# Linear-attention layers: the two bias matmuls of a key or query fill as a pair of 32-row groups

## The chip, the cores and the metric

The kernel runs on one core of one Trainium2 chip. The metric is the device time in microseconds (us). The engines are PE (TensorE matmul), DVE (VectorE), ACT (ScalarE), POOL (GpSimd) and SP (SyncE, which here only issues transfers). PEld is TensorE's weight load; it runs beside PE.

## The reference

Two transformer layers with adaptive layer norm. The change touches only the attention of the second, eight linear-attention layers on 4096 tokens (16 sequences of 256), 16 heads of 64, model size 128. One layer:

```python
Q  = elu(x @ Wq + bq) + 1                 # [tokens, 1024]
Kf = elu(x @ Wk + bk) + 1
V  = x @ Wv + bv
KV, sumK = sum(Kf * V, axis=1), sum(Kf, axis=1)      # over the tokens of a sequence
att = Q * KV / (Q * sumK + 1e-6)
x = layer_norm(gelu(att @ Wo + bo) + x)
h = gelu(gelu(x @ W1 + b1) @ W2 + b2)
x = layer_norm(h + x)
```

The biases bq and bk are not small (spread 2.0), so they are added in full precision: each is split into three bf16 parts whose sum is the bias.

## The kernel before, in words

`stack_phase` runs the eight layers. Its unit of work is 512 tokens (two sequences); there are 8 units in a layer and 64 in all. Five stages of successive units overlap in one `step`: A (keys, queries and the first half of the sums) of unit t, B (the rest of the sums, and three quarters of the output projection) of unit t-1, C (the last quarter, gelu, layer norm) of t-2, Dn (first feed-forward matmul) of t-3, E (second, layer norm, state written back) of t-4. The order on each engine is written out by hand in its own `step`, and the engines meet at counting semaphores.

For each unit, `keys(t, s, q)` runs four times (q = 0 to 3, each 128 tokens x 1024 features) and `queries(t, s, q)` four times (each 256 features x 512 tokens). Each fills two PSUM banks of 512 columns, `k_ps` or `q_ps`. In a bank three passes with split fp32 operands (hi x hi, hi x lo, lo x hi) are summed, and a fourth matmul adds the bias: the bf16 tile `b3`, 128 rows of which only rows 0 to 2 hold the three parts and the rest hold zeros, against the ones in `ones_b`. So a fill is eight matmuls, of which the fourth and the eighth are the bias. The eighth raises `k_filled` or `q_filled`.

After that ACT takes the exponential of both banks (`exp_keys`, `exp_queries`), and DVE makes the features (`feature_k`; `feature_q` in two instructions) and raises `k_ready` or `q_ready`, for which the next fill of the same banks waits. There is one pair of banks for keys and one for queries.

In a full step PE's order is: keys 0, queries 0, second feed-forward, first feed-forward 0, project 3, first feed-forward 1, sums, first feed-forward 2 and 3, sums, two groups of transposes, **keys 1**, sums, **queries 1**, sums, keys 2, queries 2, transposes, sums, project 0, sums, keys 3, transposes, project 1, queries 3, project 2. `project` q waits for the q-th `attention` of DVE, and that for the reciprocals of ACT (`log_z`, `exp_z`). DVE's order from queries 1 on is: feature_q 1, normalise, sums, attention 0, feature_k 2, sums, attention 1, sums, normalise, feature_q 2, a cast, attention 2, feature_k 3, feature_q 3, attention 3.

At each layer's end (`closing`, seven times in the loop, and once at the start for layer 0) the weights and the bias of the next layer are put in place by `swap`: for keys (k = 0) between feature_k 3 and feature_q 3 of DVE, for queries (k = 1) behind feature_q 3. DVE's part is a copy of three rows x 1024 of `raw_b3` into `b3`, and the subtraction that makes `wqk_lo`. SP loads `raw_qk` and `raw_b3` (from `bias_dram`, [8, 3, 2048]) a layer ahead, three transfers that all count on `raw_qk_in`.

In `causal_attention_phase`, long before the stack, `heads` multiplies with operands of 64 rows: two matmuls, on rows 0 to 63 and on rows 64 to 127, go to two banks one behind the other. The last phase has one matmul on 32 rows (line 2200).

Of the kernel before, what the change touches and what calls it, by code (L numbers as in the profile page):

```python
# [16 lines left out]
BF16 = mybir.dt.bfloat16  # L17
# [6 lines left out]
P = 128  # L24
# [4 lines left out]
CH = HEADS * VAL  # L29
# [11 lines left out]
def start_counters(eng, sems):  # L41

    for s in sems:
        eng.sem_inc(s, 1)
# [1205 lines left out]
def stack_phase(nc, sem, d, g):  # L1250
# [18 lines left out]
    UNIT = 4 * P  # L1269
# [4 lines left out]
    with ExitStack() as ctx:  # L1274
        sb = lambda n, s, t=F32: ctx.enter_context(nc.sbuf_tensor(n, s, t))
# [5 lines left out]
        raw_1 = sb("t_raw_1", [P, FF])  # L1281
        raw_2 = sb("t_raw_2", [P, NF, D])
        raw_ln = sb("t_raw_ln", [P, 2, D])
        raw_b3 = sb("t_raw_b3", [3, 2 * CH], BF16)

        wqk_hi = sb("t_wqk_hi", [P, 2, CH], F32R)
        wqk_lo = sb("t_wqk_lo", [P, 2, CH], F32R)
# [7 lines left out]
        b3 = sb("t_b3", [P, 2 * CH], BF16)  # L1295
        ones_b = sb("t_ones_b", [P, 4 * P], BF16)
# [6 lines left out]
        x_hi = sb("t_x_hi", [P, 2, UNIT], F32R)  # L1303
        x_lo = sb("t_x_lo", [P, 2, UNIT], F32R)
# [23 lines left out]
        k_ps = ps("t_k_ps", [P, CH])  # L1328
        q_ps = ps("t_q_ps", [P, 2 * UNIT])
# [11 lines left out]
        c = {n: sem("t_" + n) for n in names}  # L1341
# [20 lines left out]
        @block.sync  # L1362
        def _(sp):
            start_counters(sp, c.values())
            sp.sem_inc(c["state_t_ready"], PER)
            sp.sem_inc(c["state_ready"], PER)
            sp.dma_start(params[:], d["params"]).then_inc(const_in, 16)
            sp.dma_start(bv_all[:], d["bv"]).then_inc(const_in, 16)
            with sp.Fori(0, LAYERS) as n:

                once, twice, each_chunk = sp.snap(n + 1), sp.snap(2 * n + 1), sp.snap(NC * n + 1)
                sp.wait_ge(c["wqk_ready"], twice)
                sp.sem_inc(free_seen, 1)
                sp.wait_ge(c["b3_ready"], twice)
                sp.sem_inc(free_seen, 1)
                sp.dma_start(raw_qk[:, 0, :], d["wk"][bass.ds(n, 1), :, :].rearrange("a p c -> (a p) c")).then_inc(c["raw_qk_in"], 16)
                sp.dma_start(raw_qk[:, 1, :], d["wq"][bass.ds(n, 1), :, :].rearrange("a p c -> (a p) c")).then_inc(c["raw_qk_in"], 16)
                sp.dma_start(raw_b3[:], g["bias_dram"][bass.ds(n, 1), :, :].rearrange("a p c -> (a p) c")).then_inc(c["raw_qk_in"], 16)
                sp.wait_ge(c["wv_ready"], once)
                sp.sem_inc(free_seen, 1)  # L1380
                sp.wait_ge(c["bv_dot_ready"], each_chunk)
                sp.sem_inc(free_seen, 1)
                sp.dma_start(raw_v[:], d["wv"][bass.ds(n, 1), :, :, :].rearrange("a p k c -> (a p) k c")).then_inc(c["raw_v_in"], 16)
                sp.dma_start(raw_ln[:], d["ln_before"][bass.ds(n, 1), :, :].rearrange("a k c -> (a k) c").partition_broadcast(P)).then_inc(c["raw_v_in"], 16)
                sp.wait_ge(c["wo_ready"], once)
                sp.sem_inc(free_seen, 1)
                sp.dma_start(raw_o[:], d["wo"][bass.ds(n, 1), :, :, :].rearrange("a p k c -> (a p) k c")).then_inc(c["raw_o_in"], 16)
                sp.wait_ge(c["w1_ready"], once)
                sp.sem_inc(free_seen, 1)
                sp.dma_start(raw_1[:], d["w1"][bass.ds(n, 1), :, :].rearrange("a p c -> (a p) c")).then_inc(c["raw_1_in"], 16)  # L1390
                sp.wait_ge(c["w2_ready"], once)
                sp.sem_inc(free_seen, 1)
                sp.dma_start(raw_2[:], d["w2"][bass.ds(n, 1), :, :, :].rearrange("a p k c -> (a p) k c")).then_inc(c["raw_2_in"], 16)

        @block.tensor
        def _(pe):
# [3 lines left out]
            def keys(t, s, q):  # L1400

                pe.wait_ge(c["k_ready"], 4 * t + q + 1)
                for half in range(2):
                    out, cols = k_ps[:, half * 512:(half + 1) * 512], slice(half * 512, (half + 1) * 512)
                    x = slice(q * P, (q + 1) * P)
                    pe.matmul(out, x_hi[:, s, x], wqk_hi[:, 0, cols], start=True, stop=False)  # L1406
                    pe.matmul(out, x_hi[:, s, x], wqk_lo[:, 0, cols], start=False, stop=False)
                    pe.matmul(out, x_lo[:, s, x], wqk_hi[:, 0, cols], start=False, stop=False)
                    last = pe.matmul(out, ones_b[:, 0:P], b3[:, cols], start=False, stop=True)  # L1409
                last.then_inc(c["k_filled"], 1)  # L1410

            def queries(t, s, q):

                pe.wait_ge(c["q_ready"], 4 * t + q + 1)
                for k in range(2):
                    out = q_ps[:, k * UNIT:(k + 1) * UNIT]
                    lo = (2 * q + k) * P
                    pe.matmul(out, wqk_hi[:, 1, lo:lo + P], x_hi[:, s, :], start=True, stop=False)  # L1418
                    pe.matmul(out, wqk_hi[:, 1, lo:lo + P], x_lo[:, s, :], start=False, stop=False)  # L1419
                    pe.matmul(out, wqk_lo[:, 1, lo:lo + P], x_hi[:, s, :], start=False, stop=False)  # L1420
                    last = pe.matmul(out, b3[:, CH + lo:CH + lo + P], ones_b[:], start=False, stop=True)  # L1421
                last.then_inc(c["q_filled"], 1)

            def sums(t, n, k):
# [119 lines left out]
        def _(act):  # L1544
# [13 lines left out]

            def swap(layer, k):

                act.wait_ge(c["raw_qk_in"], 48 * layer + 49)
                act.activation(wqk_hi[:, k, :], raw_qk[:, k, :], ACT.Copy).then_inc(c["wqk_hi_ready"], 1)

            def exp_keys(t, q):
# [94 lines left out]
        def _(dve):  # L1659
# [3 lines left out]
            def swap(layer, k):  # L1663

                cols = slice(k * CH, (k + 1) * CH)
                dve.wait_ge(c["raw_qk_in"], 48 * layer + 49)
                dve.tensor_copy(b3[0:3, cols], raw_b3[:, cols]).then_inc(c["b3_ready"], 1)
                dve.wait_ge(c["wqk_hi_ready"], 2 * layer + k + 2)
                dve.tensor_tensor(wqk_lo[:, k, :], raw_qk[:, k, :], wqk_hi[:, k, :].bitcast(F32), ALU.subtract).then_inc(c["wqk_ready"], 1)

# [574 lines left out]
def program(nc, d, out):  # L2245
    with ExitStack() as ctx:
# [33 lines left out]
        def block1(sem):  # L2280
            with ExitStack() as ctx:
                local = lambda n, s: ctx.enter_context(nc.sbuf_tensor(n, s, F32))
                g["state_t"] = local("state_t", [P, TOKENS // (4 * P), 4 * P])
                g["state"] = local("state", [P, TILES, D + 1])
                stack_entry_phase(nc, sem, d, g)
                stack_phase(nc, sem, d, g)
                stack_exit_phase(nc, sem, d, g)
            top2_phase(nc, sem, d, g)
            store_phase(nc, sem, g, out)
# [50 lines left out]
```

## Time and profile before

| | |
|---|---|
| median of 3 runs | 4040.78 us (4039.62, 4040.78, 4046.01) |
| profiled execution: span from first to last instruction | 4045.9 us; its own time is the 4046.01 of the runs |
| PE / DVE / ACT / POOL busy | 83% / 69% / 56% / 17% |
| stack phase | about 1188 to 3745 us of the span, 64 units |
| a unit in mid-layer | 39.0 us |
| bias matmuls | 1024 (512 for keys, 512 for queries) |

An engine's busy time is the union of its instructions. Matmuls overlap in the records: a 512-column matmul is recorded with 390 to 400 ns, while the next one starts 230 to 240 ns after it. So the cost of a matmul in a stream is the distance from start to start, and not its recorded duration.

### The profile page before, as it was taken

To read this page: it belongs to the slowest core of one execution; us is meant where nothing else is said; L and a number is where in the kernel's file an instruction comes from. 1 tells how busy PE (TensorE), PEld (TensorE's weight loads), DVE (VectorE), ACT (ScalarE), POOL (GpSimd) and SP (SyncE) were. 2 spreads that over 40 slices of the span, in tenths; PEclk is the share of its full clock that TensorE was granted. 3 is DMA by queue.
4 is the path that set the end of the run, shared out by engine and by line. 5 is a ranking of instruction groups with operands and counts; after the bars stand their busy time and mean duration, and the time that the engine had idled before them with its cause. 6 is when DMAs were issued, how large, how long until landed. Compare 5 with 4: busy or idle time off the path is not lost. (4 is left out here: it accounts for less than half of the span.)

```text
span 4045.9 us, 56998 instructions
## 1 busy us (share of the span) xinstructions
PE 3365.3 (83%) x18213; PEld 2365.0 (58%) x18213; DVE 2807.3 (69%) x8434; ACT 2276.1 (56%) x3608; POOL 669.9 (17%) x826
## 2 busy tenths in 40 slices
PE   6998999513339999999999999999999999999664
PEld 5777777413226656666666666565656666666343
DVE  4556555466237787778787778787878777878566
ACT  3444444201127777777676777676767777677420
POOL 0000000104420111112111212111211111211122
PEclk9999999756659999999999999999999999999866
DMA  1000000002310000000000000000000000000000
GB/s 45 0 0 0 0 0 0 14 8 91 41 56 1 1 18 9 4 11 12 7 1 23 7 1 23 7 1 18 9 4 18 9 4 1 1 1 1 6 0 21
DMA packets 31214, 47.81 MB, mean 12 GB/s; under 512 B 3824, under 2 KB 21296, under 8 KB 30960
## 3 DMA queue, kind: packets, MB, share of 16 engines
q1 hardware_dynamic: 25328, 40.52, 3.1%
q0 software_dynamic: 5632, 4.20, 0.8%
q8 instruction: 124, 2.03, 0.2%
q14 instruction: 130, 1.06, 0.1%
HBM read 36.22 MB, written 8.49 MB: 11 GB/s over the span
## 5 line engine op out<-in xcount | busy, mean ns | idle before, releaser
L1432 PEld LDWEIGHTS t_sum_ps<-state,t_feat_k 128*128 128x128 f32 x4096 | 510.2, 192 | 79.2 <-DVE t_kv L1714 54.2
L1443 PE MATMUL t_o_ps<-t_feat_q,t_wo 128*128 128x512 f32 x1024 | 491.7, 603 | 64.0 <-DVE t_feat_q L1702 64.0
L1582 ACT ACTIVATE t_recip<-t_feat_q,t_z_eps,t_sum_k 128x256 f32<-128x256 f32 x1024 | 529.0, 590 | 24.4 <-DVE t_kv_out L1768 14.7
L1432 PE MATMUL t_sum_ps<-state,t_feat_k 128*128 128x129 f32 x4096 | 528.6, 277 | 16.0 <-DVE t_kv L1714 16.0
L1702 DVE SCALAR_TENSOR_TENSOR t_feat_q<-t_feat_q,t_kv_out,t_recip 128x256 f32<-128x256 f32 x1024 | 512.6, 561 | 6.7 <-ACT t_recip L1590 6.7
L1684 DVE SCALAR_TENSOR_TENSOR t_feat_k<-t_exp_k,t_k_ps 128x1024 f32<-128x1024 f32 x256 | 311.1, 1215 | 195.7 <-ACT t_exp_k L1567 195.7
L1567 ACT ACTIVATE t_exp_k<-t_k_ps,t_minus_one 128x1024 f32<-128x1024 f32 x256 | 283.3, 1107 | 274.7 <-PE t_k_ps L1409 274.7
L1572 ACT ACTIVATE t_exp_q<-t_q_ps,t_minus_one 128x1024 f32<-128x1024 f32 x256 | 284.0, 1109 | 186.4 <-PE t_q_ps L1421 186.4
L1418 PE MATMUL t_q_ps<-t_x_hi,t_wqk_hi 128*128 128x512 f32 x512 | 307.2, 600 | 47.6 <-DVE t_feat_q L1690 39.4
L1406 PE MATMUL t_k_ps<-t_wqk_hi,t_x_hi 128*128 128x512 f32 x512 | 289.8, 566 | 42.0 <-POOL t_x_lo L1854 24.0
L1690 DVE SCALAR_TENSOR_TENSOR t_feat_q<-t_exp_q,t_q_ps 128x1024 f32<-128x1024 f32 x256 | 312.6, 1221 | 8.8
L1443 PEld LDWEIGHTS t_o_ps<-t_feat_q,t_wo 128*128 128x128 f32 x1024 | 180.1, 191 | 213.5 <-issue 123.5
L1590 ACT ACTIVATE t_recip<-t_recip 128x1024 f32<-128x1024 f32 x256 | 270.5, 1056 | 6.2
L1714 DVE CUSTOM_DVE_ANT_0 t_junk<-t_sum_ps,t_wv 128x128 f32<-128x128 f32 x1024 | 242.4, 283 | 0.0
L273 ACT ACTIVATE a_probs<-a_pair,a_negmax 128x128 f32<-128x128 f32 x256 | 94.9, 371 | 261.4 <-DVE a_negmax L366 261.4
L1476 PE MATMUL t_m<-t_hid,t_w 128*128 128x512 f32 x512 | 234.8, 602 | 1.9 <-ACT state_t L1649 1.9
L1872 POOL TENSOR_TENSOR t_x_lo<-t_x,t_x_hi 128x512 fp32r<-128x512 f32 x64 | 92.9, 1451 | 799.0 <-DVE t_x_hi L1793 799.0
L1847 POOL TENSOR_TENSOR t_var_eps<-t_moments,t_ln_eps 128x4 f32<-128x4 f32 x128 | 25.7, 201 | 1159.7 <-DVE t_moments L1725 1159.7
L1745 DVE TENSOR_TENSOR t_y<-t_y,t_x 128x512 f32<-128x512 f32 x64 | 44.3, 692 | 242.6 <-ACT t_y L1612 242.6
L1688 DVE TENSOR_SCALAR t_exp_q<-t_exp_q 128x1024 f32<-128x1024 f32 x256 | 181.1, 707 | 39.0 <-ACT t_exp_q L1572 38.7
L1420 PE MATMUL t_q_ps<-t_x_hi,t_wqk_lo 128*128 128x512 f32 x512 | 206.4, 403 | 0.0
L1419 PE MATMUL t_q_ps<-t_x_lo,t_wqk_hi 128*128 128x512 f32 x512 | 205.6, 402 | 0.0
(355 smaller groups left out, 7550.2 us busy)
## 6 DMA issues: line engine op xcount, KB each, us to landing
t_raw_qk<-in_wk SPq DMA_DIRECT2D x8, 512.0 KB
t_raw_qk<-in_wq SPq DMA_DIRECT2D x8, 512.0 KB
t_raw_v<-in_wv SPq DMA_DIRECT2D x8, 512.0 KB, 3.4
t_raw_o<-in_wo SPq DMA_DIRECT2D x8, 512.0 KB, 3.5
t_raw<-in_w SPq DMA_DIRECT2D x16, 256.0 KB, 2.9
x<-in_x SPq DMA_DIRECT2D x4, 512.0 KB, 7.2
tokens_dram<-r_hn SPq DMA_DIRECT2D x8, 256.0 KB, 2.3
e_w_raw<-in_fc_w SPq DMA_DIRECT2D x4, 512.0 KB, 4.2
```

The costliest lines, as they stand in the source:

```text
L1406: pe.matmul(out, x_hi[:, s, x], wqk_hi[:, 0, cols], start=True, stop=False)
L1418: pe.matmul(out, wqk_hi[:, 1, lo:lo + P], x_hi[:, s, :], start=True, stop=False)
L1432: last = pe.matmul(sum_ps[:, at * (D + 1):(at + 1) * (D + 1)], feat_k[:, 2 * n + i, chunk * P:(chunk + 1) * P], rows, start=(i == 0), stop ...
L1443: last = pe.matmul(o_ps[:], wo[:, chunk, :], feat_q[:, s, chunk, :], start=(chunk == 0), stop=(chunk == NC - 1), skip_group_check=True)
L1567: act.activation(exp_k[:], k_ps[:], ACT.Exp, bias=minus_one[:, 0:1]).then_inc(c["k_exp"], 1)
L1572: act.activation(exp_q[:], q_ps[:], ACT.Exp, bias=minus_one[:, 0:1]).then_inc(c["q_exp"], 1)
L1582: last = act.activation(recip[:, q % 2, k * UNIT + n * SEQ:k * UNIT + (n + 1) * SEQ], feat_q[:, s, chunk, cols], ACT.Ln, bias=z_eps[:, 0:1 ...
L1590: act.activation(recip[:, q % 2, :], recip[:, q % 2, :], ACT.Exp, scale=-1.0).then_inc(c["recip_ready"], 1)
L1684: dve.scalar_tensor_tensor(feat_k[:, q, :], exp_k[:], 1.0, k_ps[:], ALU.min, ALU.max).then_inc(c["k_ready"], 1)
L1690: dve.scalar_tensor_tensor(feat_q[:, s, 2 * q:2 * q + 2, :], exp_q[:].rearrange("p (k t) -> p k t", k=2), 1.0, q_ps[:].rearrange("p (k t) ...
L1702: last = dve.scalar_tensor_tensor(a, a, kv_out[:, s, n, chunk:chunk + 1], recip[:, q % 2, k * UNIT + n * SEQ:k * UNIT + (n + 1) * SEQ], AL ...
L1714: last = dve.tensor_tensor_reduce(junk[:, i, :], sum_ps[:, i * (D + 1):i * (D + 1) + D], wv[:, chunk, :], 1.0, 0.0, ALU.mult, ALU.add, kv[ ...
```

## The change

Each fill issues the six fp32 passes of its two banks first and the two bias matmuls behind them. The bias matmul of bank 0 reads rows 0 to 2 of `b3` and `ones_b`, that of bank 1 reads rows 32 to 34: two groups of 32 rows of the array, neither of the full 128. `b3` and `raw_b3` hold the bias twice, at rows 0 and 32, so SP issues one more small transfer in each layer and DVE copies twice in each `swap`.

```diff
-        raw_b3 = sb("t_raw_b3", [3, 2 * CH], BF16)
+        raw_b3 = sb("t_raw_b3", [P, 2 * CH], BF16)
...
-                sp.dma_start(raw_b3[:], g["bias_dram"][bass.ds(n, 1), :, :].rearrange("a p c -> (a p) c")).then_inc(c["raw_qk_in"], 16)
+                for half in range(2):
+                    sp.dma_start(raw_b3[32 * half:32 * half + 3, :], g["bias_dram"][bass.ds(n, 1), :, :].rearrange("a p c -> (a p) c"))\
+                      .then_inc(c["raw_qk_in"], 16)
...  (keys; the three passes of each half only gain skip_group_check=True)
-                    last = pe.matmul(out, ones_b[:, 0:P], b3[:, cols], start=False, stop=True)
+                for half in range(2):
+                    rows = slice(32 * half, 32 * half + 3)
+                    last = pe.matmul(k_ps[:, half * 512:(half + 1) * 512], ones_b[rows, 0:P], b3[rows, half * 512:(half + 1) * 512],
+                                     start=False, stop=True, skip_group_check=True)
...  (queries)
-                    last = pe.matmul(out, b3[:, CH + lo:CH + lo + P], ones_b[:], start=False, stop=True)
+                for k in range(2):
+                    rows, lo = slice(32 * k, 32 * k + 3), CH + (2 * q + k) * P
+                    last = pe.matmul(q_ps[:, k * UNIT:(k + 1) * UNIT], b3[rows, lo:lo + P], ones_b[rows, :],
+                                     start=False, stop=True, skip_group_check=True)
...  (swap of ACT and of DVE)
-                act.wait_ge(c["raw_qk_in"], 48 * layer + 49)
+                act.wait_ge(c["raw_qk_in"], 64 * layer + 65)
...
-                dve.wait_ge(c["raw_qk_in"], 48 * layer + 49)
-                dve.tensor_copy(b3[0:3, cols], raw_b3[:, cols]).then_inc(c["b3_ready"], 1)
+                dve.wait_ge(c["raw_qk_in"], 64 * layer + 65)
+                for half in range(2):
+                    rows = slice(32 * half, 32 * half + 3)
+                    last = dve.tensor_copy(b3[rows, cols], raw_b3[rows, cols])
+                last.then_inc(c["b3_ready"], 1)
```

## Rows read from the trace of the kernel before

**Rows 1.** The page's part 1: busy us (share of the span) and instructions of each engine.

```profile
PE 3365.3 (83%) x18213; PEld 2365.0 (58%) x18213; DVE 2807.3 (69%) x8434; ACT 2276.1 (56%) x3608; POOL 669.9 (17%) x826
```

**Rows 2.** Busy time by stage: PE, PEld, DVE, ACT, POOL; then clock, DMA, GB/s.

```profile
1188.00:3745.00 2557.00, 2406.27 (x11349) 1581.73 (x11350) 2002.68 (x6243) 1826.23 (x2459) 453.95 (x546) 0.99 0.03 8
...
1988.43:2004.28 15.85, 14.80 (x74) 9.56 (x72) 15.78 (x46) 14.22 (x21) 3.35 (x4) 1.00 0.00 0
2009.87:2048.88 39.01, 37.73 (x181) 24.87 (x180) 30.71 (x98) 28.77 (x40) 6.65 (x8) 1.00 0.00 1
```

**Rows 3.** Groups of instructions by line, PE: busy us, mean ns, idle before, releaser.

```profile
L1443 PE MATMUL t_o_ps<-t_feat_q,t_wo 128*128 128x512 f32 x1024 | 491.7, 603 | 64.0 <-DVE t_feat_q L1702 64.0
...
L1421 PE MATMUL t_q_ps<-t_ones_b,t_b 128*128 128x512 bf16 x512 | 203.4, 397 | 0.0
L1409 PE MATMUL t_k_ps<-t_b,t_ones_b 128*128 128x512 bf16 x512 | 202.1, 395 | 0.0
```

**Rows 4.** Timeline of PE, queries 0 of a mid-layer unit: start us, duration us.

```profile
2008.72 0.39 PE L1421 MATMUL t_q_ps<-t_ones_b,t_b 128*128 128x512 bf16 x1
...
2009.65 0.39 PE L1421 MATMUL t_q_ps<-t_ones_b,t_b 128*128 128x512 bf16 x1
```

**Rows 5.** Timeline of PE in the attention phase: 128 rows, 64 rows, 128 rows.

```profile
503.22 0.39 PE L431 MATMUL a_misc<-ident,a_xn 128*128 128x128 f32 x2
503.54 0.49 PE L486 MATMUL a_pair<-a_kv_t,a_q_t 64*128 64x128 f32 x4
503.86 0.60 PE L489 MATMUL a_pair<-a_kv_t,a_q_t 64*128 64x256 f32 x4
504.39 0.40 PE L493 MATMUL a_pair<-mask,ident_b 128*128 128x128 bf16 x4
```

**Rows 6.** Timeline of PEld (weight loads) over the same stretch.

```profile
503.53 0.30 PEld L486 LDWEIGHTS a_pair<-a_kv_t,a_q_t 64*128 64x128 f32 x4 [0.17 <-issue]
...
504.39 0.23 PEld L493 LDWEIGHTS a_pair<-mask,ident_b 128*128 128x128 bf16 x4 [0.33 <-issue]
```

**Rows 7.** Single lines over the whole run: duration ns min/median/max.

```profile
L486 PE MATMUL a_pair<-a_kv_t,a_q_t x512: 272/322/374, 43.0 to 728.9; 64*128 64x128 f32 x171
...
L489 PE MATMUL a_pair<-a_kv_t,a_q_t x512: 376/377/378, 43.3 to 729.2; 64*128 64x256 f32 x171
...
L493 PE MATMUL a_pair<-mask,ident_b x512: 219/219/230, 43.8 to 729.7; 128*128 128x128 bf16 x171
```

**Rows 8.** Timeline of PE, ACT and DVE, mid-layer unit, keys 1 to project 2.

```profile
1982.39 0.48 PE L1406 MATMUL t_k_ps<-t_wqk_hi,t_x_hi 128*128 128x512 f32 x1
...
1987.28 1.11 ACT L1572 ACTIVATE t_exp_q<-t_q_ps,t_minus_one 128x1024 f32<-128x1024 f32 x1 [1.11 <-PE t_q_ps L1421]
...
1988.43 0.69 DVE L1688 TENSOR_SCALAR t_exp_q<-t_exp_q 128x1024 f32<-128x1024 f32 x1 [0.62 <-ACT t_exp_q L1572]
...
2004.34 1.98 PE L1443 MATMUL t_o_ps<-t_feat_q,t_wo 128*128 128x512 f32 x4 [0.94 <-DVE t_feat_q L1702]
```

**Rows 9.** Timeline of DVE and PE at a layer's end (swap).

```profile
2122.31 0.41 DVE L1667 COPY t_b<-t_raw_b 3x1024 bf16<-3x1024 bf16 x1
...
2122.64 1.21 DVE L1669 TENSOR_TENSOR t_wqk_lo<-t_raw_qk,t_wqk_hi 128x1024 fp32r<-128x1024 f32 x1
...
2123.98 0.49 PE L1406 MATMUL t_k_ps<-t_wqk_hi,t_x_hi 128*128 128x512 f32 x1 [0.69 <-DVE t_wqk_lo L1669]
...
2127.22 0.50 PE L1418 MATMUL t_q_ps<-t_x_hi,t_wqk_hi 128*128 128x512 f32 x1 [1.12 <-DVE t_wqk_lo L1669]
```

**Rows 10.** The same view of SP, start of the stack phase.

```profile
1171.51 0.27 SPq L1378 DMA_DIRECT2D t_raw_b<-bias_dram  x1
```

**Rows 11.** Timeline of PE in the last phase: 32 rows, then 128 rows.

```profile
3954.03 2.07 PE L2200 MATMUL m_bias_ps<-m_w_bias,m_weights_t 32*128 32x512 f32 x2 [2.14 <-ACT m_weights_t L2064]
3956.03 0.80 PE L2186 MATMUL m_out_ps<-m_w_hi,m_h_hi 128*128 128x512 f32 x1
3956.62 0.63 PE L2187 MATMUL m_out_ps<-m_w_lo,m_h_hi 128*128 128x512 f32 x1
```

More of the change, by code:

```diff
@@ L1405, in keys @@
                     x = slice(q * P, (q + 1) * P)
-                    pe.matmul(out, x_hi[:, s, x], wqk_hi[:, 0, cols], start=True, stop=False)
-                    pe.matmul(out, x_hi[:, s, x], wqk_lo[:, 0, cols], start=False, stop=False)
-                    pe.matmul(out, x_lo[:, s, x], wqk_hi[:, 0, cols], start=False, stop=False)
-                    last = pe.matmul(out, ones_b[:, 0:P], b3[:, cols], start=False, stop=True)
+                    pe.matmul(out, x_hi[:, s, x], wqk_hi[:, 0, cols], start=True, stop=False, skip_group_check=True)
+                    pe.matmul(out, x_hi[:, s, x], wqk_lo[:, 0, cols], start=False, stop=False, skip_group_check=True)
+                    pe.matmul(out, x_lo[:, s, x], wqk_hi[:, 0, cols], start=False, stop=False, skip_group_check=True)
+                for half in range(2):
+                    rows = slice(32 * half, 32 * half + 3)
+                    last = pe.matmul(k_ps[:, half * 512:(half + 1) * 512], ones_b[rows, 0:P], b3[rows, half * 512:(half + 1) * 512],
+                                     start=False, stop=True, skip_group_check=True)
                 last.then_inc(c["k_filled"], 1)
@@ L1417, in queries @@
                     lo = (2 * q + k) * P
-                    pe.matmul(out, wqk_hi[:, 1, lo:lo + P], x_hi[:, s, :], start=True, stop=False)
-                    pe.matmul(out, wqk_hi[:, 1, lo:lo + P], x_lo[:, s, :], start=False, stop=False)
-                    pe.matmul(out, wqk_lo[:, 1, lo:lo + P], x_hi[:, s, :], start=False, stop=False)
-                    last = pe.matmul(out, b3[:, CH + lo:CH + lo + P], ones_b[:], start=False, stop=True)
+                    pe.matmul(out, wqk_hi[:, 1, lo:lo + P], x_hi[:, s, :], start=True, stop=False, skip_group_check=True)
+                    pe.matmul(out, wqk_hi[:, 1, lo:lo + P], x_lo[:, s, :], start=False, stop=False, skip_group_check=True)
+                    pe.matmul(out, wqk_lo[:, 1, lo:lo + P], x_hi[:, s, :], start=False, stop=False, skip_group_check=True)
+                for k in range(2):
+                    rows, lo = slice(32 * k, 32 * k + 3), CH + (2 * q + k) * P
+                    last = pe.matmul(q_ps[:, k * UNIT:(k + 1) * UNIT], b3[rows, lo:lo + P], ones_b[rows, :],
+                                     start=False, stop=True, skip_group_check=True)
                 last.then_inc(c["q_filled"], 1)
```

## The prediction, made before the changed kernel was run

> **What bounds the kernel now.** I read the busy times first: PE leads with 83%, ahead of DVE with 69% [rows 1]. A share over the whole span says little, so I read the stages next. In the stack phase, 2557 us long and the only place that the change touches, PE is busy 94% of the time, at a granted clock of 0.99 of the full 2.4 GHz; a mid-layer unit is 39.01 us with PE busy 37.73 [rows 2]. So PE bounds most of it, but not all: PE stands idle where it waits for DVE, above all ahead of project 2 (64.0 us in the phase) [rows 3], 0.94 us in each unit [rows 8]. The reader should see two kinds of stretch, because the change is worth something different in each.
>
> *Stretch D, set by DVE.* The last bias of queries 1 raises `q_filled`; ACT, which had waited 1.11 us for it, takes the exponential at 1987.28, DVE (0.62 us idle) follows at 1988.43, and project 2 starts at 2004.34 behind DVE [rows 8]. Between 1988.43 and 2004.28 DVE is busy 15.78 of 15.85 us [rows 2]. So project 2 comes 17.1 us after queries 1 is filled, whatever PE does in between, as long as its 0.94 us of slack holds.
>
> *Stretch P, set by PE.* From project 2 on PE runs back to back: keys 0, queries 0, feed-forward, sums, until keys 1 of the next unit. The remaining piece, keys 1 to the fill of queries 1, is again PE alone. Keys 2, queries 2, keys 3 and queries 3 lie inside stretch D.
>
> **The change, part by part.** *Removed.* From one bias matmul to the next, four matmuls later, are 0.93 us [rows 4], so a slot is 0.2325 us, and the two biases of a fill cost P = 0.465 us. There are 512 such pairs, keys and queries together [rows 3]: 238 us of PE.
>
> *Put in their place.* The trace has no pair of 32-row groups amid full matmuls, but it has pairs of 64-row groups. (a) Do they overlap? Line 489's four matmuls, two for each group, take 0.60 us in all [rows 5], each recorded with 0.377 [rows 7]; so the second two start 0.22 us behind the first two, and four matmuls fill two slots. They overlap. A pair of 512-column biases should then take one slot, 0.22. (b) What does the passage from 128 rows to 64 cost? Line 431's two take 0.39 at 0.275 each: the second starts at 503.335, 0.11 a slot, so it is through at 503.445. The weights for the 64-row matmul are loaded at 503.53 and not before [rows 5, 6]. That is 0.09 us in which the array drains. (c) And back? Line 489's second two start at 504.46 - 0.377 = 504.08 and are through at 504.30; the weights of line 493 are loaded at 504.39: again 0.09. (d) In a stream the weight load hides behind the matmul before. Behind a drain it can't. Line 486's first matmul lasts 374 ns where later ones last 272: 0.10 us for fp32 weights; line 493 (bf16) 230 against 219: 0.01 [rows 7].
>
> So the time from the end of the sixth pass to the pair's results is A = 0.09 + 0.01 + 0.22 = 0.32, and the way back to full fp32 matmuls is B = 0.09 + 0.10 = 0.19. A + B = 0.51 against P = 0.465. For PE alone each pair is 0.045 us dearer, over 512 pairs 23 us: the halved streaming (0.22 to 0.25 saved) is eaten by two drains and an exposed weight load.
>
> The Trainium skill, page "TensorEngine Tiling (Array Packing)", section "Key Properties", says that a change of the tiling mode drains TensorE, whereas a change of tile within a mode doesn't. Rows 5 and 6 agree, with 0.09 us each way. The page gives no figure; without the rule the sum would go by A = 0.22 and B = 0, which is a rival below.
>
> *What of it lies on the path.* The fill's semaphore comes earlier even where the pair is dearer: P - A = 0.145 us earlier, since B falls behind it. Per unit:
> - keys 1: A + B - P = +0.045, on the path of PE to queries 1;
> - queries 1: A - P = -0.145, as stretch D starts with its semaphore;
> - keys 2, queries 2, keys 3, queries 3: inside stretch D, 0. They use up at most 4 x 0.045 = 0.18 of the 0.94 us in front of project 2;
> - keys 0 and queries 0 in stretch P: 2 x 0.045 = +0.09.
>
> Sum 4A + 3B - 4P = 1.28 + 0.57 - 1.86 = -0.01 us for a unit, about -1 us over 64 units. I count the units at the layers' ends in the same way.
>
> *Swap.* DVE copies twice. A copy is recorded with 0.41 us, but the next instruction starts 0.33 behind its start (2122.31, 2122.64), so each added copy costs 0.33. It isn't hidden: PE waits for this chain twice at a layer's end, 0.69 us ahead of keys 0 and 1.12 ahead of queries 0 [rows 9], and DVE goes from the one swap to the other without a pause. So queries 0 is 0.66 us late in each of the 7 swaps in the loop: +4.6 us. What is late next is the rest of the unit, as stretch P is back to back.
>
> *Transfers.* One more of 12 KB in each layer. In the loop it is issued a layer ahead: nothing. At the phase's start it stands on SP's queue ahead of raw_v, for which POOL and then PE wait: its issue is 0.27 us and to the next one it is some 0.5, between 0 and 0.7; I take +0.4 [rows 10]. The number of matmuls stays as it is.
>
> **Total**: -1 + 4.6 + 0.4 = +4 us on the profiled 4046.0 us (span 4045.9), which is 5.2 above the median of the three. On the median of 4040.8 that makes 4045.
>
> *Bounds.* The drains are measured for 64 rows at full clock. For 32 rows there is line 2200 at the low clock (1.2 GHz): its second matmul starts at 3956.10 - 1.056 = 3955.04, streams 0.85 (twice the 0.43 that line 1443's four are apart at full clock, (1.98 - 0.10 - 0.60) / 3, [rows 3, 8]), and the next weights follow at 3956.03: 0.13, and line 2186 then lasts 0.80 against 0.63 behind it, 0.17 for the load [rows 11]. If these held at full clock: A = 0.36, B = 0.30, sum 1.44 + 0.90 - 1.86 = +0.48 a unit, +31 us. From below: the drain of a 512-column fp32 pass may lie partly inside its own slot (512 columns at 2.4 GHz are 0.213 us, the slot is 0.2325); if half of each drain and of the exposed load were hidden, A = 0.275, B = 0.145, sum -0.33 a unit, -21 us. I stay with the 64-row rows, since they have the same clock and neighbours of the same kinds.
>
> **The rivals.**
> 1. *Passage dearer* (slower side). The bf16 weights of three rows may load as slowly as fp32 ones when the array is split; no row shows it. Then A = 0.41, sum +0.35 a unit, +22 us, total +27: 4068. The same place, dearer drains as in rows 11, gives up to +36: 4077. It decides from 4A + 3B above 2.0, that is from 0.02 more on each of the seven terms. For it: rows 11; against: rows 5 to 7. A kin of it: if the earlier semaphores gained nothing, all 23 us of PE count, +28.
> 2. *Drains cheaper* (faster side): -21 + 5 = -16 us, 4025. For it the spare 0.02 of a slot, worked out above; against it that rows 5 and 6 show 0.09 both ways.
> 3. *No passage cost at all*: A = 0.22, B = 0, sum -0.98 a unit, -63 + 5 = -58 us, 3983. Rows 5 and 6 speak against it, but for 64 rows.
> 4. *The two groups don't run together*: A = 0.54, sum +0.87 a unit, +56 + 5 = +61, 4102. PE's own extra of 8 x 0.265 = 2.1 us a unit would then also use up the slack in stretch D, which gives about the same. Against it rows 5; for it only that three rows are no full group.
>
> The Trainium skill, page "TensorE: Matmul & The Clock Gate", section "Part 3: Packing small matmuls — row/col tiling", gives matmuls in separate row groups starts about 4 ns apart, and a threefold gain for four of 32 rows with 512 columns. It counts no passage from and to full matmuls, and by it alone the result would be rival 3's; rows 5 agree on the overlap (four matmuls in two slots), and rows 6 show the passage.
>
> **How the numbers follow.** 0.2% is 8 us, about what a measurement of this kernel tells from no change. Forecast (total between -4 and +12 us; 4037 to 4053): 0.42. Rival 1: 0.27. Rival 2: 0.20. Rival 3: 0.05. Rival 4: 0.06. Faster takes rival 3 and most of rival 2, 0.23; slower takes rivals 1 and 4 and the upper edge of the forecast, 0.38; the rest, 0.39, is the same. The range reaches from rival 2 to rival 1's upper end, 4020 to 4077; it leaves out rivals 3 and 4 and a little of the edges, some 0.15.
>
> **What would show it.** In the timeline of a fill: six passes at 0.23, then weights for the bias 0.09 behind the sixth slot, two bias matmuls that start within some 10 ns, and the next full weights about 0.31 later. In ACT's waits for the fills: shorter by about 0.1. The unit's period: 39.0 +- 0.1. The wait ahead of project 2: between 0.6 and 0.94 us. At the layers' ends: two copies in each swap and PE's wait ahead of keys 0 about 0.3 longer. I am wrong if the two biases start 0.2 apart (rival 4), if the weights for the bias are loaded before the sixth pass is through (rivals 2, 3), or if the load's 0.1 shows up in the bias matmul (rival 1).

## The result, and the profile after

The changed kernel takes a median of 4054.0 us (4046.5 to 4058.3, 9 runs) against 4045.9 us (4039.1 to 4048.5, 9 runs) of the kernel before, on the same chip. The ratio is 1.0021, with a 95% interval of 1.0012 to 1.0031: some 8 us slower (5 to 12.5), on the line of what can be told from no change. The profiled execution took 4054.3 us, with a span of 4052.6.

The page's part 1 of the changed kernel, against [rows 1], and the busy times of a mid-layer unit (columns as in [rows 2]):

```profile
PE 3346.0 (83%) x18213; PEld 2346.4 (58%) x18213; DVE 2816.0 (69%) x8450; ACT 2277.8 (56%) x3608; POOL 673.9 (17%) x826
```

```profile
2014.09:2053.17 39.08, 37.57 (x183) 24.68 (x181) 30.72 (x98) 28.79 (x40) 6.72 (x8) 1.00 0.00 1
```

PE is busy 19 us less and the kernel takes longer. Half of the 19 us doesn't come from the change. Here are the windows of the stack phase and of what lies behind its last fill, in the changed kernel, and then the latter in the kernel before (its stack phase is in [rows 2]; columns as there):

```profile
1188.00:3760.00 2572.00, 2396.46 (x11349) 1573.14 (x11350) 2010.40 (x6257) 1827.81 (x2459) 457.85 (x546) 0.99 0.03 8
3760.00:4053.00 293.00, 169.12 (x524) 101.55 (x522) 176.37 (x643) 75.14 (x140) 71.21 (x97) 0.73 0.03 9
```

```profile
3745.00:4046.00 301.00, 178.21 (x524) 110.64 (x524) 176.79 (x643) 75.42 (x141) 71.25 (x97) 0.71 0.03 9
```

Behind the last fill, where both kernels do the same, PE's busy time is 9 us less, at a granted clock of 0.73 against 0.71; in the stack it is 10 us less. There PE waits longer for DVE than before, as the timelines below show. The cost of a pair is in neither number: a pass is recorded with 0.39 us, while the pair behind it starts 0.325 after it, so the records overlap and no idle time shows. The unit's period tells more than its busy time: 39.08 us here, 39.01 in [rows 2].

Groups of PE by line, over the whole run (columns as in [rows 3]):

```profile
L1451 PE MATMUL t_o_ps<-t_feat_q,t_wo 128*128 128x512 f32 x1024 | 492.0, 603 | 71.8 <-DVE t_feat_q L1713 71.8
...
L1428 PE MATMUL t_q_ps<-t_ones_b,t_b 3*128 3x512 bf16 x512 | 100.9, 390 | 0.0
```

The busy time of the 512 biases of the queries has fallen from 203.4 to 100.9 us: two biases now lie on top of each other. So the two groups do run together, and yet the kernel isn't faster.

The timeline of PE from the last pass of keys 0 on, over the two pairs that follow each other in a mid-layer unit (keys 0, then queries 0), and then the next matmul:

```profile
2011.53 0.39 PE L1410 MATMUL t_k_ps<-t_wqk_hi,t_x_lo 128*128 128x512 f32 x1
2011.85 0.39 PE L1413 MATMUL t_k_ps<-t_b,t_ones_b 3*128 3x512 bf16 x2
2012.17 0.50 PE L1423 MATMUL t_q_ps<-t_x_hi,t_wqk_hi 128*128 128x512 f32 x1
2012.51 0.40 PE L1424 MATMUL t_q_ps<-t_x_lo,t_wqk_hi 128*128 128x512 f32 x1
2012.74 0.40 PE L1425 MATMUL t_q_ps<-t_x_hi,t_wqk_lo 128*128 128x512 f32 x1
...
2013.44 0.40 PE L1425 MATMUL t_q_ps<-t_x_hi,t_wqk_lo 128*128 128x512 f32 x1
2013.77 0.39 PE L1428 MATMUL t_q_ps<-t_ones_b,t_b 3*128 3x512 bf16 x2
2014.09 3.70 PE L1484 MATMUL t_m<-t_hid,t_w 128*128 128x512 f32 x8
```

And the weight loads (PEld) in the same place:

```profile
2011.85 0.09 PEld L1413 LDWEIGHTS t_k_ps<-t_b,t_ones_b 3*128 3x128 bf16 x2 [0.36 <-issue]
2012.17 0.19 PEld L1423 LDWEIGHTS t_q_ps<-t_x_hi,t_wqk_hi 128*128 128x128 f32 x1 [0.23 <-issue]
```

Read them like this. A pass starts at 2011.53; in a stream the next would start 0.235 later, at 2011.765, but the pair's weights are loaded only at 2011.85: 0.09 us. The pair's two matmuls start 3 ns apart (0.39 us for both, where one lasts 0.385). The full weights come 0.32 behind the pair's start: one slot of 0.22 for both, and 0.10 more. The first pass with these weights then holds its slot for 0.34 us instead of 0.23 (2012.17 to 2012.51, against 2012.51 to 2012.74): 0.11 for a load that no matmul hides. From pass start to pass start over the pair are 0.325 + 0.32 + 0.34 = 0.985, where a stream with two full-row biases has 4 slots, 0.93: +0.055.

The timeline of a mid-layer unit against [rows 8], keys 1 to keys 1 of the next unit:

```profile
2025.75 0.48 PE L1408 MATMUL t_k_ps<-t_wqk_hi,t_x_hi 128*128 128x512 f32 x1
...
2030.57 1.12 ACT L1580 ACTIVATE t_exp_q<-t_q_ps,t_minus_one 128x1024 f32<-128x1024 f32 x1 [1.17 <-PE t_q_ps L1428]
...
2031.72 0.69 DVE L1699 TENSOR_SCALAR t_exp_q<-t_exp_q 128x1024 f32<-128x1024 f32 x1 [0.68 <-ACT t_exp_q L1580]
...
2047.63 1.12 PE L1451 MATMUL t_o_ps<-t_feat_q,t_wo 128*128 128x512 f32 x2 [1.08 <-DVE t_feat_q L1713]
...
2064.81 0.48 PE L1408 MATMUL t_k_ps<-t_wqk_hi,t_x_hi 128*128 128x512 f32 x1
```

Keys 1 to the exponential of queries 1: 4.82 us, where [rows 8] has 4.89. From there to project 2: 17.06, as before. The whole unit: 39.06. From starts like these I made a table for every kernel. Each entry is a mean over the seven turns of the loop, which runs from a layer's fifth unit to the next layer's fourth. The first four columns are of the turn's second unit (keys 1 to the exponential of queries 1; from there to project 2; the rest, from project 2 to the next keys 1; the period). Two more columns are the periods of the unit at the layer's end, with the swap, and of the one behind it, which opens the next layer. The unit at the turn's end is left out, as it scatters by 1.4 us or more in every kernel:

| kernel | keys 1 to exp | stretch D | rest | period | swap unit | opening unit |
|---|---|---|---|---|---|---|
| before | 4.881 | 17.048 | 17.078 | 39.007 | 41.292 | 46.151 |
| after | 4.811 | 17.059 | 17.193 | 39.063 | 42.380 | 46.740 |

Four of a turn's eight units, those without a swap and without a long wait, are 0.06 to 0.09 us longer than before, 0.07 on average; the one two behind the opening unit is 0.02 shorter.

The layer's end in the changed kernel, DVE and PE, against [rows 9]:

```profile
2126.71 0.84 DVE L1677 COPY t_b<-t_raw_b 3x1024 bf16<-3x1024 bf16 x2
2127.58 1.23 DVE L1680 TENSOR_TENSOR t_wqk_lo<-t_raw_qk,t_wqk_hi 128x1024 fp32r<-128x1024 f32 x1
...
2128.93 0.50 PE L1408 MATMUL t_k_ps<-t_wqk_hi,t_x_hi 128*128 128x512 f32 x1 [1.24 <-DVE t_wqk_lo L1680]
...
2132.73 0.50 PE L1423 MATMUL t_q_ps<-t_x_hi,t_wqk_hi 128*128 128x512 f32 x1 [1.81 <-DVE t_wqk_lo L1680]
```

The subtraction starts 0.87 us behind the first copy, where it was 0.33 behind the only one. PE's two waits went from 0.69 and 1.12 to 1.24 and 1.81 us. The swap unit is 1.09 us longer: seven of them are 7.6 us, most of the result.

### The profile page after: what moved, and what is told of

The parts are those of the page before. It is cut to its first block and busy times, and to the rows that moved or that the text cites. A ratio compares the mean times of both kernels' runs of the same rounds, so it can differ in the third digit from the quotient of the medians.

```text
span 4052.6 us, 57030 instructions
## 1 busy us (share of the span) xinstructions
PE 3346.0 (83%) x18213; PEld 2346.4 (58%) x18213; DVE 2816.0 (69%) x8450; ACT 2277.8 (56%) x3608; POOL 673.9 (17%) x826
## 5 line engine op out<-in xcount | busy, mean ns | idle before, releaser
L1451 PE MATMUL t_o_ps<-t_feat_q,t_wo 128*128 128x512 f32 x1024 | 492.0, 603 | 71.8 <-DVE t_feat_q L1713 71.8
L1440 PE MATMUL t_sum_ps<-state,t_feat_k 128*128 128x129 f32 x4096 | 538.9, 280 | 12.4 <-DVE t_kv L1725 6.0
L1423 PE MATMUL t_q_ps<-t_x_hi,t_wqk_hi 128*128 128x512 f32 x512 | 251.0, 490 | 54.4 <-DVE t_feat_q L1701 41.7
L1408 PE MATMUL t_k_ps<-t_wqk_hi,t_x_hi 128*128 128x512 f32 x512 | 240.1, 469 | 46.1 <-POOL t_x_lo L1865 23.5
```

The lines of the kernel that those rows point to most:

```text
L1440: last = pe.matmul(sum_ps[:, at * (D + 1):(at + 1) * (D + 1)], feat_k[:, 2 * n + i, chunk * P:(chunk + 1) * P], rows, start=(i == 0), stop ...
L1451: last = pe.matmul(o_ps[:], wo[:, chunk, :], feat_q[:, s, chunk, :], start=(chunk == 0), stop=(chunk == NC - 1), skip_group_check=True)
```

## The experiments

All kernels compute the whole reference. The ratio is against the kernel before in the same batch: 4049.9 us for the first four kernels (27 runs), 4052.4 for the last three (21 runs).

| kernel | what it is | median us (runs) | ratio, 95% interval |
|---|---|---|---|
| e1_one_copy | the change, with one copy in each swap | 4052.7 (11) | 1.0007 [0.9996, 1.0018] |
| e2_order_only | before, biases behind the six passes | 4048.1 (10) | 0.9995 [0.9985, 1.0005] |
| e3_one_group | the change, both biases in one row group | 4121.3 (4) | 1.0173 [1.0156, 1.0191] |
| e4_copy_twice | before, with the second copy alone | 4057.9 (11) | 1.0023 [1.0013, 1.0032] |
| e5_pair_at_q1 | pairs at queries 1 alone | 4050.7 (11) | 0.9992 [0.9983, 1.0001] |
| e6_pair_but_0 | pairs but at keys 0 and queries 0 | 4045.8 (11) | 0.9986 [0.9976, 0.9996] |
| e7_q1_and_order | pairs at queries 1, elsewhere e2's order | 4039.1 (5) | 0.9964 [0.9951, 0.9978] |

And the unit's stretches, in the same columns as above:

| kernel | keys 1 to exp | stretch D | rest | period | swap unit | opening unit |
|---|---|---|---|---|---|---|
| e1 | 4.813 | 17.064 | 17.187 | 39.065 | 41.286 | 45.751 |
| e2 | 4.854 | 17.060 | 17.042 | 38.957 | 41.265 | 45.977 |
| e3 | 5.229 | 17.223 | 17.637 | 40.089 | 42.077 | 48.621 |
| e4 | 4.888 | 17.058 | 17.076 | 39.022 | 42.391 | 46.469 |
| e5 | 4.751 | 17.121 | 17.073 | 38.945 | 41.218 | 46.129 |
| e6 | 4.822 | 17.061 | 17.075 | 38.957 | 41.215 | 45.847 |
| e7 | 4.738 | 17.092 | 17.038 | 38.868 | 41.177 | 45.695 |

### The two parts of the change apart: one copy (e1), two copies (e4)

e1 is the change with one copy over 35 rows, so that the pair stays and the second copy goes. The rows between the two biases are cleared once, at the start.

```diff
-                for half in range(2):
-                    rows = slice(32 * half, 32 * half + 3)
-                    last = dve.tensor_copy(b3[rows, cols], raw_b3[rows, cols])
-                last.then_inc(c["b3_ready"], 1)
+                dve.tensor_copy(b3[0:35, cols], raw_b3[0:35, cols]).then_inc(c["b3_ready"], 1)
```

> The changed kernel with one DVE copy of rows 0 to 34 in each swap in place of two copies of three rows (raw_b3 is zeroed once at the start, by DVE). Theory (the pair of row groups costs 0.07 us a unit, the second copy of each swap 0.54 us): the unit at a layer's end falls from 42.39 to about 41.3 us, mid-layer units stay at 39.08, the total falls by 14 x 0.54 = 7.6 us, to about that of the kernel before (+1 to +5). Rival (the eight microseconds are PE's dearer pairs): the layer-end unit falls too, but the total stays within 3 us of the changed kernel's.

e4 is the kernel before, with the second copy and nothing else; the matmuls keep all rows, so `ones_b` is 1 in rows 0 to 2 and 0 below.

```diff
-                dve.tensor_copy(b3[0:3, cols], raw_b3[:, cols]).then_inc(c["b3_ready"], 1)
+                for half in range(2):
+                    last = dve.tensor_copy(b3[32 * half:32 * half + 3, cols], raw_b3[:, cols])
+                last.then_inc(c["b3_ready"], 1)
```

> The kernel before with a second copy of three rows in each DVE swap (to rows 32 to 34 of b3, which the ones, set to zero from row 3 on, leave out of the sums). Theory: the layer-end unit goes from 41.29 to 42.4 us, the other units stay, total +7.7 us. Rival (the copy is hidden behind other waits, and the layer-end unit grew for another reason, such as the row groups): layer-end unit up by less than 0.3 us, total within 3 us of before.

Measured: e4's mid-layer unit is the old one (39.02 against 39.01) and its swap unit 1.10 longer; the whole kernel is 0.23% slower, interval 0.13 to 0.32%. e1's swap unit is the old one (41.29 against 41.29) and its mid-layer unit the changed one (39.07 against 39.06); the whole is 0.07% slower, within the uncertainty. The totals of e1 and of the changed kernel were measured in different batches, and their intervals overlap, so they don't refute e1's rival by themselves; the swap units and e4 do. So the copy alone costs what the whole change costs, as far as the totals can tell, and the pairs at most 7 us.

The timelines at the layer's end show where the 1.1 us come from, instead of the 0.66 that I had. First e4, DVE and PE:

```profile
2125.62 0.84 DVE L1669 COPY t_b<-t_raw_b 3x1024 bf16<-3x1024 bf16 x2
2126.49 1.23 DVE L1672 TENSOR_TENSOR t_wqk_lo<-t_raw_qk,t_wqk_hi 128x1024 fp32r<-128x1024 f32 x1
...
2127.85 0.49 PE L1407 MATMUL t_k_ps<-t_wqk_hi,t_x_hi 128*128 128x512 f32 x1 [1.24 <-DVE t_wqk_lo L1672]
```

Then e1, the same place:

```profile
2127.87 0.41 DVE L1678 COPY t_b<-t_raw_b 35x1024 bf16<-35x1024 bf16 x1
2128.21 1.21 DVE L1680 TENSOR_TENSOR t_wqk_lo<-t_raw_qk,t_wqk_hi 128x1024 fp32r<-128x1024 f32 x1
...
2129.55 0.49 PE L1410 MATMUL t_k_ps<-t_wqk_hi,t_x_hi 128*128 128x512 f32 x1 [0.69 <-DVE t_wqk_lo L1680]
```

A single copy lets the subtraction start 0.34 behind its start, while it is itself recorded with 0.41: the two overlap by 0.07. Of two copies, the second starts 0.42 behind the first, and the subtraction 0.45 behind the second: nothing overlaps. The second copy costs 0.53 us in each swap, not 0.33. A copy of 35 rows lasts as long as one of 3.

The Trainium skill, page "VectorE: DVE Perf Modes", section "Two Vector instructions with no wait between them", has the rule that fits: an instruction whose output (or input) starts in another group of 32 partitions than the last one's is held until every earlier one has finished. The copy to row 32 is such a step, and the subtraction, which goes back to row 0, is the next. e4 and e1 agree with it: in e4 only the output changes its group, and both gaps are there; in e1 all start at row 0, and neither is. No run had the second copy in the same group, so what is shown is that two copies at rows 0 and 32 cost this; that the change of group is the cause is that rule of the Trainium skill, and not shown here.

### The order alone (e2)

```diff
+                for half in range(2):
+                    last = pe.matmul(k_ps[:, half * 512:(half + 1) * 512], ones_b[:, 0:P], b3[:, half * 512:(half + 1) * 512],
+                                     start=False, stop=True, skip_group_check=True)
```

It is the kernel before, with the biases behind the six passes, over all 128 rows; queries likewise; swap and transfers as before.

> The kernel before with the order of the changed one: six passes, then the two biases, both over all 128 rows, so no row groups. Theory (only the passage between row groupings and the overlap matter): mid-layer units at 39.01 us as before, total within 0.1% of before; the fill's semaphore is not earlier. Rival (the order of passes and biases itself moves the time, for example through weight loads that hide better or worse when fp32 passes stand together): mid-layer units move by more than 0.1 us.

Measured: the period is 38.96, 0.05 less than before (0.04 on average over the four ordinary units of a turn), and the exponential of queries 1 comes 0.03 earlier; in the whole no difference that can be measured, 0.9995 [0.9985, 1.0005]. So theory (39.01, no earlier semaphore) and rival (more than 0.1) both missed by a little. The order costs nothing; its 0.04 is a gain that my sum didn't have, and against this order the pairs cost 0.11 us a unit, not 0.07. Why it gains was not taken apart.

### Two biases in one row group (e3)

```diff
-                    rows = slice(32 * half, 32 * half + 3)
+                    rows = slice(0, 3)
```

It has the passage from and to full rows, but the two can't overlap; swap and transfer are those of before.

> The changed kernel with both biases of a fill on rows 0 to 2, that is in the same group of 32 rows, and the single copy and transfer of before. Theory (drain 0.09, one slot, drain 0.09, exposed load 0.10; two groups overlap): the two biases start 0.22 us apart, a pair costs 0.27 us more than in full rows, a mid-layer unit is 0.9 us longer than before (39.9), total +56 us. Rival (the row groups' overlap buys nothing, only the earlier semaphore counts): less than +20 us.

The timeline of PE at queries 0:

```profile
2039.49 0.40 PE L1423 MATMUL t_q_ps<-t_x_hi,t_wqk_lo 128*128 128x512 f32 x1
2039.82 0.60 PE L1426 MATMUL t_q_ps<-t_ones_b,t_b 3*128 3x512 bf16 x2
2040.35 1.12 PE L1482 MATMUL t_m<-t_hid,t_w 128*128 128x512 f32 x2
```

The two take 0.60 instead of 0.39, so they start 0.22 apart; the way in (0.33 from the last pass's start) is the same, and the next full matmul comes 0.53 behind, not 0.32. The unit is 40.09 (+1.08), the whole 1.73% slower (+70 us; +63 to +77), more than the 56 I had expected. The formula gives +0.87 a unit; the missing 0.2 is mostly stretch D, which grew from 17.05 to 17.22. It grew before project 2 comes into play: PE's sums behind project 0 start 9.05 us behind the exponential instead of 8.83, and DVE's copy of them 10.14 instead of 9.99 (medians of the seven units), while PE still waits 0.86 us ahead of project 2. So the overlap is real and worth about 1.0 us a unit, and it is what pays for the passages.

### Pairs only where they pay: e5, e6, e7

By the terms of the prediction a pair pays in one place, at the end of a piece that something waits for (queries 1), and costs wherever PE runs on. e6 keeps the pairs but at keys 0 and queries 0, which lie in stretch P; e5 keeps only queries 1; e7 is e5 with the full-row biases behind the six passes, as in e2. All have e1's one copy. The core of e5:

```diff
+                if q in (0, 2, 3):
+                    last = pe.matmul(out, b3[:, CH + lo:CH + lo + P], ones_3[:], start=False, stop=True, skip_group_check=True)
+                else:
+                    last = pe.matmul(q_ps[:, k * UNIT:(k + 1) * UNIT], b3[rows, lo:lo + P], ones_b[rows, :], start=False, stop=True, skip_group_check=True)
```

(This is the last step of `queries`; in `keys` all four take the first branch. `ones_3` is 1 in rows 0 to 2 and 0 below, as `b3` holds the bias twice now. In e6 the condition is `q in (0,)` in both functions.)

> Row groups at keys 1 to 3 and queries 1 to 3; keys 0 and queries 0 as in the kernel before. One copy in each swap. Theory: the +0.125 us that the changed kernel has between project 2 and the next keys 1 is gone, the -0.07 between keys 1 and the exponential of queries 1 stays (4.81), keys 2, 3 and queries 2, 3 cost nothing: mid-layer unit 38.94, total -4.5 us against before. Rival (pairs cost PE wherever they stand): 39.05 or more, total +3.

> Row groups at queries 1 alone; the other seven fills of a unit have their biases over all 128 rows and in the order of the kernel before (their ones are zero from row 3 on, since b3 holds the bias twice). One copy in each swap. Theory (a pair saves 0.13 to 0.145 us up to the fill's semaphore and costs 0.055 only where PE must go on at once; queries 1 starts a stretch that DVE sets, and what PE does behind it has slack): from keys 1 to ACT's exponential of queries 1 4.76 us against 4.89 before, all other stretches as before, mid-layer unit 38.88 against 39.01, total -8 us. Rival (a pair costs its 0.055 wherever it stands): unit 39.06, total +3.

> As the kernel with row groups at queries 1 alone, and in the other seven fills both full-row biases stand behind the six passes, which was worth 0.045 us a unit by itself. Theory: the two add up, mid-layer unit 38.84, total -10 us against before. Rival (the order's gain was in queries 1 and is already in it): 38.88, total -8.

e6 came out as the terms have it: the rest of the unit is back to 17.075 (before 17.078), the exponential still 0.06 earlier, the unit 0.05 shorter than before and 0.11 shorter than e1's; the whole 0.9986 [0.9976, 0.9996].

e5 shows a limit of them. The exponential comes at 4.751, 0.13 earlier, as expected; but of that only 0.06 arrives. Stretch D has grown by 0.07. Timeline of ACT and PE in e5, and then in e7:

```profile
2033.73 1.11 ACT L1602 ACTIVATE t_exp_q<-t_q_ps,t_minus_one 128x1024 f32<-128x1024 f32 x1 [0.97 <-PE t_q_ps L1450]
2034.04 1.60 PE L1462 MATMUL t_sum_ps<-state,t_feat_k 128*128 128x129 f32 x12 [0.35 <-DVE t_kv L1748]
```

```profile
2029.31 1.11 ACT L1607 ACTIVATE t_exp_q<-t_q_ps,t_minus_one 128x1024 f32<-128x1024 f32 x1 [0.97 <-PE t_q_ps L1455]
2029.62 1.61 PE L1467 MATMUL t_sum_ps<-state,t_feat_k 128*128 128x129 f32 x12 [0.35 <-DVE t_kv L1753]
```

PE, earlier now, waits 0.35 us for `t_kv` behind the fill, where before it waits 0.20. DVE makes `t_kv` behind feature_k 1, which hangs on the fill of keys 1, and that is no earlier in e5. So PE starts its sums 0.31 us behind the exponential instead of 0.16. The timeline shows what comes of it, PE's sums behind project 0 and DVE's copy of them, e5 and then before:

```profile
2042.68 1.06 PE L1462 MATMUL t_sum_ps<-state,t_feat_k 128*128 128x129 f32 x8
2043.78 0.16 DVE L1745 COPY t_sum_k<-t_sum_ps 128x2 f32<-128x2 f32 x1
```

```profile
1996.09 1.06 PE L1432 MATMUL t_sum_ps<-state,t_feat_k 128*128 128x129 f32 x8
1997.27 0.15 DVE L1711 COPY t_sum_k<-t_sum_ps 128x2 f32<-128x2 f32 x1
```

Counted from the exponential, PE's sums start at 8.95 instead of 8.81, and DVE's copy at 10.05 instead of 9.99; up to this copy DVE keeps its old distances, and from it on all is 0.06 late. The copy waits for the sums: in e5, e7 and e3 it starts 1.09 us behind them (medians), in before 1.16. So PE has 0.07 us of slack at this place, and not the 0.94 in front of project 2. In the changed kernel and in e6 the pair at keys 1 brings `t_kv` forward as well, PE's sums start 0.10 behind the exponential, and the pairs of keys 2 and queries 2 only use up that lead (8.84).

In the whole e5 is 0.9992 [0.9983, 1.0001], some 3 us where I expected 8. e7 adds the order and comes to 38.87 a unit and 0.9964 [0.9951, 0.9978]: 15 us by the ratio, 13 by the medians. Its theory (38.84) and its rival (38.88) both started from the 38.88 that e5 was to have; from e5's real 38.945 the order takes 0.08 off, so that it adds nothing there is refuted. It is the only version that is faster than the kernel before by more than 0.2%. The unit's 0.139 less would make 64 x 0.139 = 8.9 us of it; the opening and swap units have their part (45.70 and 41.18 against 46.15 and 41.29), and the rest isn't accounted for: it is one batch of 5 runs, and e5 and e2 apart gain only 0.08% and 0.05%.

### The unit that opens the next layer

In the profiled executions the changed kernel's opening unit is 46.74 us against 46.15, but e1 with the same pairs has 45.75. The stretch from its exponential to project 2 varies within one execution: in before it is 23.95, 24.97, 24.79, 23.68, 25.03, 23.95 and 23.5 us in the seven layers, in after 24.7 to 24.9 in all of them, in e1 23.4 to 24.1 and once 24.7. The timeline of PE in after:

```profile
2159.49 0.80 PE L1423 MATMUL t_q_ps<-t_x_hi,t_wqk_hi 128*128 128x512 f32 x1 [5.04 <-DVE t_feat_q L1701]
2160.09 0.63 PE L1424 MATMUL t_q_ps<-t_x_lo,t_wqk_hi 128*128 128x512 f32 x1
2160.51 0.63 PE L1425 MATMUL t_q_ps<-t_x_hi,t_wqk_lo 128*128 128x512 f32 x1
```

The windows behind such a wait, first after, then two layers of before (the column behind the busy times is the granted clock):

```profile
2159.40:2164.40 5.00, 4.91 (x15) 3.44 (x16) 4.73 (x17) 1.68 (x3) 0.00 (x0) 0.50 0.20 77
```

```profile
1503.80:1508.80 5.00, 4.94 (x19) 3.42 (x20) 4.69 (x17) 1.84 (x3) 0.00 (x0) 0.60 0.22 81
...
1829.40:1834.40 5.00, 4.97 (x15) 3.46 (x16) 4.66 (x16) 1.51 (x3) 0.00 (x0) 0.50 0.15 58
```

PE has idled for 5.0 us, and the granted clock is at the lower of its two levels behind it (1.2 GHz, 0.50): the passes start 0.42 apart instead of 0.23. In some layers it comes back within the 5 us (0.60 over the window, which is one fifth at full clock), in others not. In the seven layers of after it was the late return each time (24.6 us or more), which makes some 3.7 us of the profiled span and no part of my terms. Whether the change makes the late return likelier is open. It doesn't go with the pairs: before had it in 3 of 7, e1 in 1, e2, e5 and e6 in 2 each, e7 in none. The two kernels with the second copy had it often, after in 7 and e4 in 5 of 7, so it may be a further price of the copy, which stands just ahead of this unit; but e3, with one copy, had it later still in 6 of 7 (25.8 to 26.6 us). One profiled execution of each can't settle it, as the layers of one execution aren't independent of each other.

## Why the prediction was right, and where it was not

Predicted were 4045 us, 4.2 more than the median shown then, with 4020 to 4077 and the same as likeliest. The ratio puts the change at +8.1 us (5 to 12.5); on the same base that is 4049. The total lies in the forecast's own range (-4 to +12), at the 8 us that it called the bound to slower. Two terms were too small, and one came true for another reason than the stated one. By steps:

**That the pairs overlap, and the two passages eat the gain: right, shown.** The way in was 0.09, as [rows 5, 6] had it, the two biases start 3 ns apart and take one slot, the way back is 0.10 and the exposed load 0.11. e3 shows what is left if the overlap is taken away. The 64-row rows of the attention phase were the right ones to read; the ones at the low clock [rows 11] would have given +0.48 a unit, and +0.07 came. Rival 1 is refuted in its mechanism: the biases' weights took 0.09 us to load and held nothing up, and the semaphores did gain. Rivals 2, 3 and 4 are refuted by the same rows. (Rival 2's sum has a slip: with half of the exposed load hidden too, as its condition says, B would be 0.095 and the sum -0.5 a unit, not -0.33.) The rule that a change of the tiling mode drains TensorE is the Trainium skill's, "TensorEngine Tiling (Array Packing)", section "Key Properties". The trace agrees for groups of 32 rows: 0.09 and 0.10 us around each pair.

**A + B - P = +0.045: it was +0.055.** The semaphore of a fill comes 0.13 earlier, not 0.145: the exponential of keys 1 started 2.005 us behind keys 1, before 2.141.

**Where the pieces fall: right, with small misses that add up.** Keys 1 to the exponential gave -0.07 (predicted 0.045 - 0.145 = -0.10), stretch D +0.01 (0), the rest +0.12 (+0.09; e6 takes it away). So +0.06 in this unit, 0.07 on average in the four ordinary ones of a turn, where the sum had -0.01. Seven terms, each off by about 0.01 us, all with one sign, make this. One sees it at the way back: 0.10 of drain where I had 0.09, and 0.11 of load where I had 0.10. But "I count the units at the layers' ends in the same way" failed: e1's swap unit is no longer than before (41.29), since PE waits there for DVE anyway, and the unit two behind the opening one isn't longer either. So the pairs cost some 3 us in all (an estimate from the units' periods without the clock's part), where I had -1, and 64 x 0.07 would be 4.5. The measured e1 is +2.8.

**Stretch D: right by luck.** "As long as its 0.94 us of slack holds" named the wrong place. The slack that counts is the 0.07 us at the sums behind project 0, which e5, e7 and e3 overran. In the changed kernel it held because the pair at keys 1 moved `t_kv` forward, which the prediction did not have.

**The swap: the term that was mis-sized.** "Each added copy costs 0.33": it measured 0.53, and 1.10 a layer's end instead of 0.66, +7.7 us instead of +4.6. This step took the distance from the copy to its follower as the copy's price. That distance has an overlap of 0.07 in it; the new copy starts only when the first is through, and its follower only when the new one is. That it isn't hidden, and what is late next, was right: e4 shows the whole of it.

**The start: nothing.** +0.4 us was put down for the transfer ahead of `raw_v`. From SP's first issue of the phase to PE's first matmul are 19.0 us in after, where before has 19.4.

Together +3 + 7.7 + 0 = +11 us, against the measured +8.1 (5 to 12.5): inside its interval. The two parts apart give +0.07% (-0.04 to 0.18) and +0.23% (0.13 to 0.32), which is 2.8 and 9.3 us, each inside its interval too. The difference between the two profiled spans (4045.9 and 4052.6) doesn't test it: from PE's first matmul of the stack phase to its last (at 3824.1 in before, 3839.8 in after) are 15.4 us more in after, of which 3.7 are the late clock of the opening units and 1.7 the scatter at the turn's end, and what is behind the stack, which the change doesn't touch, was 9.0 us shorter.

**What I said one would see.** Three of the signs came out otherwise. PE's wait ahead of keys 0 at a layer's end was to grow by 0.3; it grew by 0.55, from the mis-sized copy. ACT's wait for queries 1 was to be 0.1 shorter; it is 1.17 against 1.11, since ACT is itself done with keys 1 0.13 earlier, and the fill only 0.07. And PE's wait ahead of project 2 was to be between 0.6 and 0.94; it is 1.08 (71.8 us in all, against 64.0). I had let four dearer pairs add up in front of it. Timeline of PE in front of project 2, after:

```profile
2042.47 0.66 PE L1540 MATMUL t_m<-ident,t_y 128*128 128x128 f32 x4 [0.29 <-DVE t_y L1741]
...
2046.16 0.39 PE L1428 MATMUL t_q_ps<-t_ones_b,t_b 3*128 3x512 bf16 x2
2047.63 0.70 PE L1451 MATMUL t_o_ps<-t_feat_q,t_wo 128*128 128x512 f32 x1 [1.08 <-DVE t_feat_q L1713]
```

The same place before:

```profile
1999.17 0.66 PE L1532 MATMUL t_m<-ident,t_y 128*128 128x128 f32 x4 [0.17 <-DVE t_y L1730]
...
2003.00 0.39 PE L1421 MATMUL t_q_ps<-t_ones_b,t_b 128*128 128x512 bf16 x1
```

PE waits for DVE once before, ahead of the transposes of `t_y`, and starts afresh there. Of the fills only queries 3 lies between the two waits, and a single pair whose way back falls into a wait is through 0.13 earlier. An earlier wait wipes out what stands in front of it; slack isn't used up by a sum over a whole stretch.

## What to carry to other kernels

Count a packed matmul amid full ones with its two passages: here a pair of 3-row, 512-column matmuls cost 0.52 us where two full-row ones cost 0.465, so a pair paid only where something waits for the fill (whether more than two that share one passage would pay, no run shows). Where a gain and a loss are within 0.05 us of each other, put the change only at the places where the gain arrives: e7, with an eighth of the pairs, one copy and e2's order, is 0.36% faster than before, the whole change 0.21% slower. Look for slack at every hand-over of a stretch and not only at its end: here it was 0.07 us and not 0.94. And price an added instruction by what it does to its neighbours' overlap (here 0.53 us for a copy whose follower used to start after 0.33), not by the gap in the old trace.

## What the runs showed of the hardware that I had not expected

- Two DVE copies of 3 x 1024 bf16 at rows 0 and 32 start 0.42 us apart, and a subtraction at row 0 starts 0.45 behind the second; behind a copy at row 0 it starts after 0.34. A copy of 35 rows lasts as long as one of 3 (0.41).
- Behind a wait of 4.9 to 5.0 us PE's granted clock was at its lower level for less than the 5 us that the window shows in some layers (0.60 on average) and for all of them in others (0.50), in the same kernel and at the same place of the loop; it moves that unit by 1.0 to 1.5 us.
- With six fp32 passes and then two full-row bf16 biases in every fill, a unit takes 0.04 to 0.05 us less than with the biases between them (e2, 38.96 against 39.01), with the same number of matmuls.
- A 0.39 us record of a matmul runs on over the drain behind it (the pair starts 0.325 us later), so PE's busy time doesn't show what a pair costs.
